# Graph network on one core: order of loads, one addition and one bias of the node stage moved between engines

## The reference

```python
# layer 0: attention over edges, then at every node
q, k, v = h @ Wq.T + bq, h @ Wk.T + bk, h @ Wv.T + bv        # h = x @ Wx.T + bx
alpha   = exp(score - segment_max) / (segment_sum + 1e-16)
m       = segment_sum((v[src] + e) * alpha, dst)
u       = tanh(h @ A.T + m + b_ac)
x1      = layernorm(x + tanh(h + u))
# layer 1: an MLP over edges, then at every node
edge    = relu(concat(x1[src], x1[dst]) @ We1 + be1) @ We2 + be2
agg     = segment_sum(edge, dst)
out     = layernorm(2 * x1 + (relu(concat(x1, agg) @ Wn1 + bn1) @ Wn2 + bn2))
```

## Time and profile before

| | |
|---|---|
| time, three runs | 4156.49, 4165.62 (median), 4168.34 us |
| time of the profiled execution | 4168.75 us |
| its span | 4166.4 us |
| instructions | 73778 |
| busy share PE, PEld, DVE, ACT, POOL | 75%, 68%, 60%, 42%, 73% |
| mean granted TensorE clock | 0.818 |

### The profile page before, as it was taken

The page is one execution under the profiler, slowest core; times in us unless marked ns, Lnnn a source line. Parts: engine busy times, 40 slices in busy tenths (PEclk is TensorE's granted clock), DMA queues, the critical chain, the costliest instruction groups (busy, mean ns, idle before and its releaser), DMA issues. The chain is left out here.

```text
span 4166.4 us, 73778 instructions
## 1 busy us (share of the span) xinstructions
PE 3109.7 (75%) x18778; PEld 2828.7 (68%) x18779; DVE 2484.7 (60%) x5456; ACT 1733.6 (42%) x2900; POOL 3021.9 (73%) x3193
## 2 busy tenths in 40 slices
PE   6888788878888888888676666666666777677776
PEld 4777777777777777777546666666666666666665
DVE  4877777777777777777574444444444445454544
ACT  3767776777677677777461111111111111111111
POOL 5777777777777777777347777777777777777775
PEclk8999999999999999999896666666666666766666
DMA  6333333333333333333234333333333333333332
GB/s 186 81 81 83 81 83 81 82 81 82 81 81 82 81 81 82 81 82 82 75 97 103 90 92 88 91 90 89 93 89 92 92 94 94 94 95 94 93 96 61
DMA packets 419860, 370.13 MB, mean 89 GB/s; under 512 B 269651, under 2 KB 347883, under 8 KB 419724
## 3 DMA queue, kind: packets, MB, share of 16 engines
q0 software_dynamic: 100032, 217.87, 20.6%
q1 hardware_dynamic: 308544, 143.31, 13.5%
q10 hardware_dynamic: 11214, 8.17, 0.7%
HBM read 347.56 MB, written 21.44 MB: 89 GB/s over the span
## 5 line engine op out<-in xcount | busy, mean ns | idle before, releaser
L721 POOL DMA_INDIRECT he<-h_table,src_i x1563 | 1482.8, 949 | 516.0 <-issue 504.3
L1637 POOL DMA_INDIRECT msg<-p_table,src x1563 | 1477.5, 945 | 484.1 <-issue 484.1
L1654 PE MATMUL p_edge<-r_win,hotT 80*128 80x128 f32 x3136 | 660.6, 396 | 586.0 <-DVE msg L1774 569.6
L1654 PEld LDWEIGHTS p_edge<-r_win,hotT 80*128 80x128 f32 x3136 | 610.3, 298 | 626.4 <-issue 525.6
L1710 ACT ACTIVATE msg<-msg 128x1024 f32<-128x1024 f32 x196 | 207.2, 1057 | 1647.9 <-DVE msg L1774 1647.9
L1774 DVE TENSOR_TENSOR msg<-msg,p_edge 128x512 f32<-128x512 f32 x392 | 251.8, 683 | 699.8 <-DMA msg<-p_table,src 699.8
L1665 PE MATMUL p_sumT<-msg,hot 128*80 128x129 f32 x3136 | 607.4, 375 | 28.7 <-ACT sumT L1718 28.7
L1665 PEld LDWEIGHTS p_sumT<-msg,hot 128*80 128x80 f32 x3136 | 586.4, 226 | 46.7 <-issue 46.6
L1764 DVE SCALAR_TENSOR_TENSOR hotT<-dst_row,start_b,p_iota 80x1024 f32<-80x1024 int32 x196 | 403.4, 2058 | 297.3 <-PE p_edge L1654 297.2
L760 PE MATMUL p_score<-qk_two,heT 128*128 128x160 f32 x1568 | 395.1, 335 | 168.4 <-ACT heT L870 167.1
L762 PE MATMUL p_score<-qk_win,heT 128*128 128x80 f32 x3136 | 462.6, 272 | 0.0
(11 more groups left out here) (205 smaller groups left out, 4118.4 us busy)
## 6 DMA issues: line engine op xcount, KB each, us to landing
dst_row<-in_dst_dram SPq DMA_DIRECT2D x196, 320.0 KB
feat<-in_edge_attr_dram SPq DMA_DIRECT2D x196, 128.0 KB
he<-h_table,src_i POOLq DMA_INDIRECT x1563
msg<-p_table,src POOLq DMA_INDIRECT x1563
qk_win<-qk_table SPq DMA_DIRECT2D x196, 40.0 KB
qk_two<-qk_table SPq DMA_DIRECT2D x392, 20.0 KB
r_win<-r_table SPq DMA_DIRECT2D x196, 40.0 KB
qk_table<-qk SPq DMA_DIRECT2D x13, 512.0 KB
```

The lines of the kernel that those rows point to most:

```text
L721: e.indirect_dma_start(out=he[u][:, j, 2 * FE:2 * FE + ROW], out_offset=None, in_=h_table[:, :], in_offset=bass.IndirectOffsetOnAxis(ap=sr ...
L1637: e.indirect_dma_start(out=msg[u][:, j, 0:D], out_offset=None, in_=p_table[:, :], in_offset=bass.IndirectOffsetOnAxis(ap=src_i[u][:, j:j + ...
L1654: mm = e.matmul(p_edge[h][:, j % 4, :], hotT[:, j, :], r_win[u][:, :], start=True, stop=True)
```

## The change

The part that only clears 13 semaphores is gone; SyncE clears them in the node stage, behind its last store. In the node stage the eight weight loads go from SyncE to ScalarE, and ScalarE's three loads of X now wait until the reciprocals are in memory (`den_io` 48). h2 is made by GpSimd, as the first of its stages. The bias be1 is loaded as one row and added by TensorE, as a product of a row of ones with it, for each of the four blocks of r; ScalarE copies r, in a stage of its own behind outs, and its copy of p goes ahead of outs. The DVE keeps pres, moments and normal.

```diff
-        with ExitStack() as c2:
-            block = c2.enter_context(nc.Block())
-            @block.sync
-            def _(e):
-                for used in early_sems[stage_sems:]:
-                    e.sem_clear(used)
-        early.close()
...
-            be1_b = sb("be1_b", [P, D], ctx=ctx)
+            be1_r = sb("be1_r", [1, D], ctx=ctx)
...
             @block.sync
                 e.dma_start(den[:, :], den_dram[0, :].rearrange("(b p) -> b p", p=P)).then_inc(den_io, 16)
-                e.dma_start(we1[:, :, :], We1.rearrange("(k p) d -> p k d", p=P)).then_inc(loads, 16)
-                e.dma_start(be1_b[:, :], be1.partition_broadcast(P)).then_inc(loads, 16)
...
-                    e.dma_start(be2_c[:, :], col(be2)).then_inc(loads, 16)
                 e.wait_ge(s["rden_done"], 1)
...
                 pipelined(e, (0, load_ahead), (3, store))
+                for used in early_sems[stage_sems:]:
+                    e.sem_clear(used)
                 for out_d in (p_out_d, r_out_d):
...
             @block.gpsimd
+                def add_update(g, k):
+                    at = place(e, g, G)
+                    n0, n1 = val(e, g), val(e, g + 1)
+                    e.wait_ge(s["upd_done"], n1)
+                    e.sem_inc(passed, 1)
+                    again(e, s["outT_done"], n0)
+                    e.sem_inc(passed, 1)
+                    e.tensor_tensor(h2[:, :], hT[:, bass.ds(at, G)], upd[:, :], ALU.add).then_inc(s["h2_done"], 1)
...
-                pipelined(e, (3, keep), (1, clear))
+                pipelined(e, (0, add_update), (3, keep), (1, clear))
...
             @block.tensor
                         for b in range(GB):
-                            mm = e.matmul(p[:, b * D:(b + 1) * D], x1T_g[k][:, b * P:(b + 1) * P], we1[:, i, :], start=True, stop=True)
+                            mm = e.matmul(p[:, b * D:(b + 1) * D], x1T_g[k][:, b * P:(b + 1) * P], we1[:, i, :], start=True, stop=(i == 0))
+                            if i == 1:
+                                mm = e.matmul(p[:, b * D:(b + 1) * D], ones[0:1, :], be1_r[:, :], start=False, stop=True)
...
             @block.scalar
+                e.dma_start(we1[:, :, :], We1.rearrange("(k p) d -> p k d", p=P)).then_inc(loads, 16)
+                e.dma_start(be1_r[:, :], row(be1)).then_inc(loads, 16)
...
+                    e.dma_start(be2_c[:, :], col(be2)).then_inc(loads, 16)
+                def copy_r(g, k):
+                    e.wait_ge(s["r_full"], val(e, g + 1))
+                    again(e, r_out_d[k], val(e, (g - k) * 8))
+                    e.sem_inc(passed, 1)
+                    e.activation(r_rows[k][:, :, :], p_r[:, :].rearrange("p (b d) -> p b d", d=D), ACT.Copy).then_inc(s["r_done"], 1)
+                e.wait_ge(den_io, 48)
                 e.dma_start(X[:, 0:XG * GB, :], x[0:XG * G, :].rearrange("(b p) d -> p b d", p=P)).then_inc(x_in[0], 16)
...
-                pipelined(e, (2, roots), (3, copy_x1), (0, update), (0, outs), (3, copy_p))
+                pipelined(e, (2, roots), (3, copy_x1), (0, update), (3, copy_p), (0, outs), (3, copy_r))
...
             @block.vector
                     e.wait_ge(s["val_full"], n1)
+                    again(e, s["pre_done"], n0)
...
-                pipelined(e, (0, pres), (1, moments), (2, normal), (0, add_update), (3, copy_r))
+                pipelined(e, (0, pres), (1, moments), (2, normal))
```

More of the change, by code:

```diff
@@ L1341, in copy_p @@
                     e.activation(p_rows[k][:, :, :], p_p[:, :].rearrange("p (b d) -> p b d", d=D), ACT.Copy).then_inc(s["p_done"], 1)
+                e.dma_start(we1[:, :, :], We1.rearrange("(k p) d -> p k d", p=P)).then_inc(loads, 16)
+                e.dma_start(be1_r[:, :], row(be1)).then_inc(loads, 16)
+                e.dma_start(wn1[:, :, :], Wn1.rearrange("(k p) d -> p k d", p=P)).then_inc(loads, 16)
+                e.dma_start(we2[:, :], We2).then_inc(loads, 16)
+                e.dma_start(wn2[:, :], Wn2).then_inc(loads, 16)
+                e.dma_start(bn2_b[:, :], bn2.partition_broadcast(P)).then_inc(loads, 16)
+                with nc.allow_non_contiguous_dma(reason="bias columns, 128 numbers each"):
+                    e.dma_start(bn1_c[:, :], col(bn1)).then_inc(loads, 16)
+                    e.dma_start(be2_c[:, :], col(be2)).then_inc(loads, 16)
[5 more added lines that the diff above has]
+                e.wait_ge(den_io, 48)
                 e.dma_start(X[:, 0:XG * GB, :], x[0:XG * G, :].rearrange("(b p) d -> p b d", p=P)).then_inc(x_in[0], 16)
@@ L1361, in pres @@
                     e.tensor_tensor(pre[:, :], p_anti[:, :], mean_v[:, :], ALU.add).then_inc(s["pre_done"], 1)
[L1363 to L1368, removed]
                 def moments(g, k):
@@ L1375, in moments @@
                         e.wait_ge(x_in[0], 16)
-                        e.wait_ge(loads, LOADS2)
                     elif isinstance(g, int) and g == XG:
@@ L1405, in normal @@
                     op.then_inc(s["xn_done"], 1)
[L1407 to L1411, removed]
                 e.wait_ge(den_io, 32)
@@ L1422, in _ @@
                 e.tensor_copy(be2n[:, :], p_w[0:1, 2 * P:3 * P])
+        early.close()
         with ExitStack() as ctx:
```

## The result

The changed kernel takes 4193.03 us (median of six runs, 4187.46 to 4200.2); the kernel before, run beside it, 4162.72 (six runs). The ratio is 1.0073, interval 1.0063 to 1.0083: **slower by 0.73%**, 30 us. The forecast was +3.6 us and no measurable change; its range ended at 4179.

A forecast was written before the change was run, and what follows sets the result against it. GpSimd gathers were taken to bound the edge layers, ScalarE's round the node loop; -3.9 (start) + 1.9 (to the fifth group) + 2.2 (loop) + 3.4 (tail) = +3.6 us, giving 4169.2 us, range 4158 to 4179.

The forecast's parts named there:

- (1): Start of the node stage: dropping the clearing part saves 1.03 us; the clears behind the last store cost 0.
- (2): Start: reciprocals out 7 us sooner, but ScalarE held by issuing X; gain 1.4 at first tanh, 3.9 at third group.
- (3): Node loop: h2 on GpSimd takes 1.48 us, making ScalarE's wait from upd to outT 1.78 instead of 1.52.
- (4): Node loop: r copy on ScalarE and p copy ahead of outT cost 0; group time 7.05, +0.28 a group.
- T: Time of one group in the node loop, upd to upd: 6.77 us before, forecast 7.05, set by ScalarE's round.
- (6): Node loop: the DVE loses 0.68 + 0.68 us a group but waits for TensorE either way, so nothing is gained.
- rival C: Node loop: the DVE was the bound, so each group falls by 1.36 us; sum -9.5, 4156 us; chance 0.04.
- (5): Node loop: eight bias passes add 0.93 us, leaving TensorE's ring at 6.77; +1.9 by the fifth group.
- (7): Tail, the last three groups without tanh: the bias passes add 3.4 us (2.8 to 4).
- Rival B: Node loop: h2 on GpSimd waits for the DVE's xn, group time 7.95; sum +10.8, 4176 us; chance 0.12.
- Rival A: Start: SyncE's eight loads, not X, held ScalarE; first tanh at 2073.7, sum +0.5, 4166 us; chance 0.17.
- D: Outside the node stage: something there moves, either way; chance 0.05.

The follow-up runs named there:

- r3: The changed kernel with bias products of 128 rows, 127 of them zero, in the same order; 4163.73 us, ratio 1.0000 to the kernel before.
- r1: The changed kernel without the bias products (be1 left out); 4163.56 us against 4165.32 for the kernel before, ratio 0.9997.
- r9: The kernel before with the new start, X's small part issued first and the p copy ahead of outs; 5208.16 us for 5224.78 on another chip, ratio 0.9968.
- r11: The changed kernel with bias products of 64 rows (be1 and zeros); 5249.73 us against 5224.78 for the kernel before, on another chip, ratio 1.0045.
- r5: The kernel before with only the one-row bias products added, the DVE copying r without adding; 4208.53 us for 4167.01, ratio 1.0097.
- r7: The changed kernel with h2 back on the DVE, behind xn; 4201.02 us, ratio 1.0078 to the kernel before.
- r2: The changed kernel with its four one-row bias products all ahead of r's four 128-row products; 4168.92 us, ratio 1.0015 to the kernel before.
- r4: The changed kernel with one bias product of 1 row and 512 columns ahead of r's four; 4167.93 us, ratio 1.0012 to the kernel before.
- r10: The changed kernel with bias products of 65 rows (be1 and zeros); 5214.4 us against 5224.78 for the kernel before, on another chip, ratio 0.9986.
- r6: The kernel before with only the change's start (no clearing part, weights on ScalarE's queue, X behind the reciprocals); 4161.82 us for 4167.01, ratio 0.9989.
- r8: The kernel before with the change's start, and X's last, small part issued ahead of the two large ones; 4157.57 us for 4167.01, ratio 0.9976.

## Why the prediction was wrong

The sum's terms, measured from the same marks:

| term | forecast | after | r3 (equal rows) |
|---|---|---|---|
| start, to the third tanh | -3.9 | -4.95 | -5.8 |
| third to fifth | +1.9 | +4.3 | +2.2 |
| (the two together) | -2.0 | -0.7 | -3.6 |
| loop, eight groups | +2.2 | +21.1 | +2.9 |
| tail | +3.4 | +13.5 | +3.3 |
| sum | +3.6 | +34.0 | +2.6 |

- **(1) clearing**: right. SyncE's first transfer starts 5.1 behind the last sum where it was 6.1, and the 13 clears now run from 2206.0 to 2206.7, ahead of the first gather at 2211.0.
- **(2) denominators first**: right in its mechanism. ScalarE was held by X (9.74 for 9.04) and the first tanh stood behind it. The terms ahead were cheaper than taken: load back 2.13 for 3.5 (2055.23 to 2057.36), reciprocals out 1.47 for 3.1 (2058.59 to SyncE's next issue at 2060.06), so X went out sooner. At the first tanh the gain was 4.1 for the 1.4 forecast, outside its bounds (-4.6 to 1.8); at the third, 4.95 for 3.9.
- **(3), (4)**: right in the number, in part by luck. h2 took 1.26 for the 1.48 taken, but started 0.37 behind upd's end for the 0.17 taken; the two cancel, and the gap was 1.78 as forecast. T of the kernel with everything but the bias is 7.07 for 7.05.
- **(6)**: wrong in its reason. The DVE's work did not fall by 1.36 a group but rose by 0.7, from 47.77 to 53.54 us in eight groups of r1, since xn was stretched; and it no longer waited for TensorE in r1. So **rival C** was not tested by the change. What speaks against it is r9: T fell by 0.29 with nothing taken off the DVE.
- **(5) the bias by TensorE**: this is the step that failed. It priced eight passes at the spacing of the 16 beside them, +0.93, and so found TensorE's ring at 6.77, still under ScalarE's. The passes cost 2.33 in that order: 0.89 for themselves (r3) and (2.33 - 0.89) / 8 = 0.18 for each of the eight changes between one row and 128; by the spacing of the pairs it is 0.415 - 0.222 = 0.19. The ring is 8.31 and takes the place of ScalarE's. With equal rows the term measured 0.89.
- **The trace of before had the price.** The bound of (5) came from 128-row products, but a one-row product stands in layer 1's last node work, L1506, which I did not read. Its timeline in before, at 2.4 GHz:

```profile
3276.77 0.60 PE L1504 MATMUL p_hid<-hT,wn 128*128 x2
3277.20 0.59 PE L1505 MATMUL p_hid<-acc,we2n 128*128 x2
3277.73 0.69 PE L1506 MATMUL p_hid<-acc,be2n 1*128 x2
```

  From one 128-row product of 256 columns to the next it is 0.43, from the second to the one-row product 0.53; from that to the 128-row product behind it 0.63 in another group (3199.93 to 3200.56, also at 2.4 GHz). That is 0.10 + 0.20 for a visit to one row, 4 x 0.3 = +1.2 a group: TensorE's ring at 5.84 + 0.93 + 1.2 = 7.97, past ScalarE's 7.05. As an estimate, the sum becomes 3.6 + 8 x 0.92 in the loop + 4 x 1.2 for the first tables and the three of the tail, where TensorE ends last = +15.8: past the 12.5 that can be told from no change, and 4181 us, past the range's end. It is still under half of the 34: a change of rows in this loop cost more (1.4 a group for 1.2), and the rest is the clock.
- **(7) the tail**: +13.5 for +3.4, by the same term, and because the tail ran at 0.50, where a step costs 0.72. With equal rows it was +3.2.
- **The clock** was no term of the sum but in (5)'s first tables and the tail. It cost 8.3 in the loop. Ahead of its fall at 2136 TensorE had been busy 24.85 of 26 us; in r11 it was busy 62.9 of 66 with the same order of products and kept 1.00. So the alternation does not bring the lower clock by itself (r11 has 64 rows for one, though, and ran on another chip). In the loop the clock fell only where one row and 128 alternate: 0.89 over the eight groups of after, r5 and r7, 1.00 in all others, r2 and r4 with one row side by side included. From the last tanh to the first gather it was 0.56 to 0.68 in every kernel with bias products of 1 or 64 rows (after, r2, r4, r5, r7, r11) and 0.84 to 0.98 in every other, r3 and r10 included. So the low clock goes with products of few rows; why **stays open**.
- **Rival B** was the right side for the wrong reason: the two do collide, but the DVE pays most, and in after off the path. It wasn't h2 that waited for four pieces of xn. **Rival A** falls with after and r6, where the loads stood elsewhere and the issue was stuck all the same. **D**: layer 1 took the same time (1984.07 for 1984.04); layer 0's 5.3 us less are in this one execution.

## What to carry to other kernels

Price a new product from a row with the same number of rows next to the same neighbours, not from the products that it joins; search the whole trace for the form, also in stages that the change does not touch. Where a small product must stand among full ones, put the small ones together (T 7.17 for 9.35), or give them the full rows with zeros (7.07). Count what an operation moved to GpSimd does to the DVE beside it: here it cost the DVE more than it took off. And where an engine that computes also issues DMAs, issue the largest last: nothing then stands behind it, and here the first tanh came 5.7 us sooner (r8 against r6).

## What the runs showed of the hardware

- Fp32 products of 128 rows and 128 columns that alternate with products of 1 or 64 rows take 0.415 us a pair of passes at 2.4 GHz (0.72 at 1.2 GHz, 1 row) instead of 0.22; with 65 rows it is 0.22 (after, r11, r10). No number of rows between 1 and 64 was run. That it is the weight load that no longer overlaps is argued from the spacing, 0.19 being about one load (184 ns on average for those of 64 rows in r11's loop); it was not shown separately. The Trainium skill's page "TensorE: Matmul & The Clock Gate", section "What happens when you issue a matmul", says that a weight load is pulled ahead of a product in flight if their row groups don't conflict or if it goes to the background buffer. No run here shows which of the two would fail at 64 rows and not at 65.
- A DMA issue on ScalarE's queue behind the 2.3 MB transfer is held for 9.04 to 11.14 us (before, r11); the large one's own issue takes 0.86 to 1.66 (before, r8).
- One 128x128 piece of DVE work between SBUF tiles went from 0.34 to as much as 1.40 us beside a GpSimd addition of 1.26 (after, against r7).
